# Per-head q and k transposes with per-head waits, in place of grouped loads with an early k, in a recurrent attention and FFN kernel

## The reference

```python
xn = layernorm(x)
q, k, v = heads(xn @ Wq), heads(xn @ Wk), heads(xn @ Wv)     # q, k rotated (rope)
beta = clip(sigmoid(xn @ Wg + bg), 0.8, 0.9995)
pq, pk = elu(q) + 1, elu(k) + 1
# for each token t and head:
S = S * b_t + pk_t (outer) v_t
z = z * b_t + pk_t
y_t = (pq_t @ S) / (sum(pq_t * z) + 1e-6)
s = y @ Wo + bo
# FFN with 8-bit weights, W = (wq - 128) * scale, hidden size 5632
g = silu( qlin( silu(qlin(xn, gate)) * qlin(xn, up), down ) )
out = x + s * g
```

## Time and profile before

| | us |
|---|---|
| two runs | 4832.46, 4834.73 |
| median of these | 4833.59 |
| the profiled execution | 4846.22 |
| its span, slowest core (2) | 4844.4 |
| its span, fastest core (5) | 4747.9 |

### The profile page before, as it was taken

The page is one execution under the profiler, slowest core; times in us unless marked ns, Lnnn a source line. Parts: engine busy times, 40 slices in busy tenths (PEclk is TensorE's granted clock), DMA queues, the critical chain, the costliest instruction groups (busy, mean ns, idle before and its releaser), DMA issues.

```text
span 4844.4 us, 44791 instructions; the slowest of 8 cores (4747.9 to 4844.4 us)
## 1 busy us (share of the span) xinstructions
PE 3282.6 (68%) x15312; PEld 1518.6 (31%) x15312; DVE 1009.8 (21%) x1735; ACT 528.2 (11%) x1021; POOL 632.2 (13%) x705
## 2 busy tenths in 40 slices
PE   0014777777761887877789888885525888638888
PEld 0012333323220433433334444443412333213333
DVE  1244435353521111111111111111400000000000
ACT  0110122222210111111111111111100000000000
POOL 0101243433320000000000000000010000100000
PEclk9997899999985988888899899897557899868899
DMA  7521132323229534355534453435394354764343
GB/s 147 140 87 23 38 75 47 79 46 78 45 67 208 114 93 114 88 116 114 105 85 106 91 118 92 91 83 122 100 161 112 105 131 125 136 129 120 104 130 96
DMA packets 661693, 491.81 MB, mean 102 GB/s; under 512 B 392928, under 2 KB 595680, under 8 KB 655328
## 3 DMA queue, kind: packets, MB, share of 16 engines
q0 software_dynamic: 67056, 173.10, 17.1%
q1 hardware_dynamic: 424944, 154.34, 14.6%
q10 hardware_dynamic: 169472, 161.52, 12.7%
HBM read 337.83 MB, written 167.77 MB: 104 GB/s over the span
## 4 chain that ended last, share of the span: by engine, by line
PE 48%; DMA 15%; DVE 11%; SPq 7%; POOL 7%; issue 7%; ACT 3%; ACTq 1%; DVEq 1%; POOLq 0%
PE pb L724 12%; PE pb L732 11%; PE pb L1060 10%; SPq L1006 6%; PE pb L985 5%; PE pb L581 4%; DMA raws<-wqu 4%; DMA raws<-wqg 4%; POOL swp L614 3%; DMA yTm<-yt_sp 2%; DMA raws<-wqd 2%; PE pb L856 2%; DVE tmp L628 2%; DVE tmp L620 2%; ACT mnb L626 2%
## 5 line engine op out<-in xcount | busy, mean ns | idle before, releaser
L724 PE MATMUL pb<-xnT,wgT 128*128 128x512 bf16 x2816 | 733.5, 420 | 104.0 <-DVE Am L805 70.9
L581 PE MATMUL pb<-ws,xnT 128*128 128x512 bf16 x2880 | 664.8, 392 | 115.0 <-DVE tmp L609 114.6
L732 PE MATMUL pb<-xnT,wuT 128*128 128x512 bf16 x2816 | 659.2, 389 | 103.9 <-DVE gub L745 87.0
L1060 PE MATMUL pb<-wdT,guTm 128*128 128x512 bf16 x2464 | 534.1, 379 | 0.0
L581 PEld LDWEIGHTS pb<-ws,xnT 128*128 128x128 bf16 x2880 | 284.4, 100 | 493.5 <-issue 188.3
L724 PEld LDWEIGHTS pb<-xnT,wgT 128*128 128x128 bf16 x2816 | 288.1, 106 | 479.5 <-issue 241.3
L732 PEld LDWEIGHTS pb<-xnT,wuT 128*128 128x128 bf16 x2816 | 280.3, 100 | 455.8 <-issue 139.2
L985 PE MATMUL pb<-wos,yTm 128*128 128x512 bf16 x960 | 272.5, 455 | 176.7 <-DMA yTm<-yt_sp 176.7
L1060 PEld LDWEIGHTS pb<-wdT,guTm 128*128 128x128 bf16 x2464 | 241.1, 98 | 290.7
L741 POOL TENSOR_TENSOR gub<-upsb,gsb 128x512 bf16<-128x512 bf16 x88 | 101.5, 1153 | 1235.0 <-ACT upsb L738 1234.8
L452 PE MATMUL pbt<-identb,xnb 128*128 128x128 bf16 x256 | 32.4, 306 | 337.2 <-DVE xnb L444 319.9
(11 more groups left out here) (110 smaller groups left out, 2200.3 us busy)
## 6 DMA issues: line engine op xcount, KB each, us to landing
guTm<-gu_sp ACTq DMA_DIRECT2D x64, 704.0 KB, 9.0
raws<-wqg POOLq DMA_DIRECT2D x11, 2048.0 KB, 19.0
wg_sp<-raws POOLq DMA_DIRECT2D x11, 2048.0 KB, 8.2
raws<-wqu POOLq DMA_DIRECT2D x11, 2048.0 KB, 15.5
wu_sp<-raws POOLq DMA_DIRECT2D x11, 2048.0 KB, 8.7
gu_sp<-gub ACTq DMA_DIRECT2D x176, 128.0 KB, 2.5
raws<-wqd POOLq DMA_DIRECT2D x16, 1408.0 KB, 13.3
wd_sp<-raws POOLq DMA_DIRECT2D x16, 1408.0 KB, 6.1
```

The costliest lines, as they stand in the source:

```text
L581: P.mm_group([(lambda e, k=k, m=m, sl=sl, pbank=pbank: e.matmul(pb[pbank][:, 0:512], xnT[:, k * L + m * 128:k * L + (m + 1) * 128], wslot[ ...
L724: P.mm_group([(lambda e, k=k, t=t, tb=tb, sl=sl: e.matmul(pb[6][:, 0:512], wgT[sl][:, k * FS + t * 128:k * FS + (t + 1) * 128], xnT[:, k * ...
L732: P.mm_group([(lambda e, k=k, t=t, tb=tb, sl=sl: e.matmul(pb[7][:, 0:512], wuT[sl][:, k * FS + t * 128:k * FS + (t + 1) * 128], xnT[:, k * ...
L1060: e.matmul(pb[pbank][:, 0:DDS], guTm[msl][:, kh * 256 + mi * 128:kh * 256 + (mi + 1) * 128], wdT[j][:, kh * DDS:(kh + 1) * DDS], start=(kh ...
```

## The change

The q and k loads of a group are written as eight single DMAs, q and k in turn for each head, at the start of the group. Each head's q and k has a buffer object and a semaphore of its own (`dqt0` to `dqt3`, `dkt0` to `dkt3`). The issue of the next group's k in chunk 15 is gone. `phase_A` consists of four matmul groups of one matmul, each waiting for its own head's q and k; numerator and denominator wait for all four heads. Tiles and arithmetic are the same.

```diff
-            qTgB, kTgB = P.buf("qTg"), P.buf("kTg")
+            qTgBh = [Buf(f"qTgh{hl}") for hl in range(HG)]
+            kTgBh = [Buf(f"kTgh{hl}") for hl in range(HG)]
...
-            def emit_q_loads(g):
-                P.dma_group("sp", [
-                    (lambda e, hl=hl, g=g: e.dma_start(
+            for g in range(NG):
+                for hl in range(HG):
+                    P.dma("sp", lambda e, hl=hl, g=g: e.dma_start(
                         qTg[:, hl * L:(hl + 1) * L],
-                        qt_sp[:, (g * HG + hl) * 128:(g * HG + hl + 1) * 128], transpose=True))
-                    for hl in range(HG)],
-                    reads=[qt_spB[m][g] for m in range(MT)], writes=[qTgB], sem="dqt")
-
-            def emit_k_loads(g):
-                P.dma_group("sp", [
-                    (lambda e, hl=hl, g=g: e.dma_start(
+                        qt_sp[:, (g * HG + hl) * 128:(g * HG + hl + 1) * 128], transpose=True),
+                        reads=[qt_spB[m][g] for m in range(MT)], writes=[qTgBh[hl]],
+                        sem=f"dqt{hl}")
+                    P.dma("sp", lambda e, hl=hl, g=g: e.dma_start(
                         kTg[:, hl * L:(hl + 1) * L],
-                        kt_sp[:, (g * HG + hl) * 128:(g * HG + hl + 1) * 128], transpose=True))
-                    for hl in range(HG)],
-                    reads=[kt_spB[m][g] for m in range(MT)], writes=[kTgB], sem="dkt")
-
-            for g in range(NG):
-                emit_q_loads(g)
-                if g == 0:
-                    emit_k_loads(0)
+                        kt_sp[:, (g * HG + hl) * 128:(g * HG + hl + 1) * 128], transpose=True),
+                        reads=[kt_spB[m][g] for m in range(MT)], writes=[kTgBh[hl]],
+                        sem=f"dkt{hl}")
...
-                    P.mm_group([(lambda e, hl=hl, c=c, bkA=bkA, kTg=kTg, qTg=qTg: e.matmul(
-                        pb[bkA][:, hl * 128:(hl + 1) * 128],
-                        kTg[:, hl * L + c * 128:hl * L + (c + 1) * 128],
-                        qTg[:, hl * L + c * 128:hl * L + (c + 1) * 128],
-                        start=True, stop=True)) for hl in range(HG)],
-                        reads=[qTgB, kTgB], writes=[pbB[bkA]])
+                    for hl in range(HG):
+                        P.mm_group([(lambda e, hl=hl, c=c, bkA=bkA: e.matmul(
+                            pb[bkA][:, hl * 128:(hl + 1) * 128],
+                            kTg[:, hl * L + c * 128:hl * L + (c + 1) * 128],
+                            qTg[:, hl * L + c * 128:hl * L + (c + 1) * 128],
+                            start=True, stop=True))],
+                            reads=[qTgBh[hl], kTgBh[hl]], writes=[pbB[bkA]])
...
-                    P.mm_group(numer_fns, reads=[stbB, qTgB, vchB[sl], AmB[cp]], writes=[pbB[bkN]])
+                    P.mm_group(numer_fns, reads=[stbB, vchB[sl], AmB[cp]] + qTgBh,
+                               writes=[pbB[bkN]])
...
-                    P.mm_group(den_fns, reads=[stbB, qTgB, AmB[cp], constsB], writes=[pbB[2]])
+                    P.mm_group(den_fns, reads=[stbB, AmB[cp], constsB] + qTgBh,
+                               writes=[pbB[2]])
...
-                    if c == NC - 1 and g + 1 < NG:
-                        emit_k_loads(g + 1)
```

More of the change, by code:

```diff
@@ L820, in phase_rest @@
                         h = g * HG + hl
-                        numer_fns.append(lambda e, hl=hl, h=h, c=c, bkN=bkN, qTg=qTg: e.matmul(
+                        numer_fns.append(lambda e, hl=hl, h=h, c=c, bkN=bkN: e.matmul(
                             pb[bkN][:, hl * 128:(hl + 1) * 128],
@@ L834, in phase_rest @@
                         h = g * HG + hl
-                        den_fns.append(lambda e, hl=hl, h=h, c=c, dco=dco, qTg=qTg: e.matmul(
+                        den_fns.append(lambda e, hl=hl, h=h, c=c, dco=dco: e.matmul(
                             pb[2][:, dco + hl:dco + hl + 1],
```

## The result

| | kernel before | changed kernel |
|---|---|---|
| median of the runs beside each other, us | 4838.7 | 4910.5 |
| ratio, with 95% interval | | 1.013 [1.0103, 1.0158] |
| profiled execution, us | 4846.2 | 4893.0 |
| its slowest core, span us | 2: 4844.4 | 7: 4891.4 |
| granted clock there | 0.859 | 0.858 |

Both medians include runs in which part of the chip ran at a lower clock; the ratio leaves such runs out, so it is the number to use. On the predicted base of 4833.6 it is +63 us, 50 to 76, or 4896 us; predicted were +53.6 and 4887. The change makes the kernel 1.3% slower, less than the 2% that the chances were put against.

What follows compares the result with a forecast made beforehand. TensorE's in-order stream in the recurrent stage was taken to bound the kernel. Late k 35.8, self-waits 14.8 and clock 3 summed to +53.6 us on 4833.6, giving 4887.2; own range 4875 to 4900, with rivals 4860 to 4924.

Steps and rivals of the forecast that it cites:

- part 1: At the three head-group changes, k leaves its early place, putting four transposes in the open each time: +35.8 us, bounds 28 to 59.
- Change 1: First head-group change: the raws load is over when the second four transposes start, so they go at the quiet rate, +11.4 us.
- Rival C: At the group changes, loads catch the added k transposes: +8 to +11 us at changes 1 and 3, 4905 to 4910; chance 0.15.
- Change 2: Second head-group change: the added four transposes fall into a raws load, FFN goes on 14 to 17 us later; taken as +13.
- The credit: At change 2: the 6.82 us stall for Am becomes short, and 2.7 us of lower clock behind it comes back.
- Change 3: Third head-group change, no FFN work left: k follows q at the quiet rate and everything after shifts, +11.4 us.
- The cover of the FFN weights: At change 2: wgT loads start up to 22 us later, yet end about 2853, before 2866.74, with 13 to spare.
- Part 2: phase_A in four groups, all 64 chunks: 192 self-waits of 0.32 us, partly covered by later waits, +14.8; bounds 8.6 to 61.
- Rival D: In phase_A, the self-wait is nearly free for 128-column matmuls: 36 to 38 us remain, 4871; chance 0.1.
- Part 3: FFN matmuls behind Am in 13 odd chunks: two fall to the lower clock, 2 x 1.7 = 3 us; bounds 0 and 35.
- Rival A: Self-waits drop the clock in most of 13 odd and six open even chunks: 32 to 51 us, about 4925; chance 0.1.
- Rival B: At the group changes, added transposes run beside the q ones for nothing, so not slower: 4835 or 4831; chance 0.04.

Runs made afterwards that it cites:

- e1: Changed kernel with phase_A as one matmul group again, so late k loads alone; ratio 1.0102 to the kernel before, stage +42 us.
- e8: Changed kernel with phase_A in one group and all four q transposes before the four k; ratio 1.0125 to the kernel before, stage +48 us.
- e5: Changed kernel with chunk 0's weight preparation put before chunk 1 instead, in groups 1 to 3; ratio 1.0138 to the kernel before.
- e11: Kernel before with preparation loads issued one job ahead, late k transposes and phase_A in one group; ratio 0.9856 to the kernel before.
- e2: Kernel before with phase_A in four groups, each waiting for TensorE's own count, loads unchanged; ratio 1.0022, stage +20 us.
- e3: Changed kernel without the waits for TensorE's own count in phase_A's matmuls 2 to 4; ratio 1.009 to the kernel before, stage +51 us.
- e12: Kernel before with preparation loads issued one job ahead and q transposed in two token halves, the first early; ratio 0.9631, median 4694 us.
- e7: Kernel before with each weight preparation's raws load issued one job ahead, into the other buffer; ratio 0.9813, stage -99 us.

## Why the prediction was right, and which step was mis-sized

**Direction and total: right.** Forecast +53.6, measured +63 [50, 76]. The mechanism was right too, with part 1 too small. The profiled execution was forecast at 4899.8 and took 4893.0.

**Part 1, the late k: right in kind, too small.** I had 35.8; e1 and e8, which have nothing else, give ratios of 1.0102 and 1.0125, 49 and 60 us, with a stage of +42 and +48. By changes:

- *Change 1, "+11.4": this is the step that failed.* The block grew by 21.9, and e1's stretch by 20.5. I had written that "the load is over by the time the second four start, so they go at the k rate", and against rival C that "DVE and POOL stand still in the stall, so no new load is issued". No new load is, but the store of the load before it is, and VectorE is free for the scaling that releases it. e5, which moves the store out, takes 5 to 8 of the extra 10 away, and in e11, where it falls on the load, the extra 10 doesn't appear. Rival C had the right mechanism at this one change (its +8 to +11), with the wrong transfer, and a smaller catch than its 13: 7.87 on core 1.
- *Change 2, "+13".* The added transposes came as worked out: predicted 19.4 to 22.4 more, measured 22.7. But FFN work went on 19.9 later by the median of eight cores, not 14 to 17, and the stretch in e1 grew by 22. The credit was too large: I took the stall for Am that goes away from the slowest core, 6.82, where the eight cores have 3.9 to 8.6, median 5.4. And the 2.7 of clock came back in part. Before, on core 2, the first gate group of the change took 5.30 and the second, behind the stall for Am, 6.32; in the changed kernel they took 5.48 and 3.61 on core 2, and 6.27 and 5.30 on core 7 (above). The second took 3.61 on six of the eight cores, and its median went from 5.30 to 3.61, so 1.7 came back. The rows of core 2, before and then changed:

```profile
2792.97 5.30 PE L724 MATMUL pb<-xnT,wgT 128*128 128x512 bf16 x16
```

```profile
2799.71 5.48 PE L724 MATMUL pb<-xnT,wgT 128*128 128x512 bf16 x16
...
2810.94 3.61 PE L724 MATMUL pb<-xnT,wgT 128*128 128x512 bf16 x16 [1.14 <-DVE Am L798]
```

- *Change 3, "+11.4".* Block +11.8, stretch +10.7 (+10.3 in e1). Right.
- The cover of the FFN weights held: on core 7 wgT was transposed from 2837.05 at 20.37, and the next span's came at 2911.77.

**Part 2, the self-waits: right.** 0.31 each instead of 0.32. Forecast 14.8, with 3 for the clock 17.8: by stage e2 costs 20, by its ratio 11 with an interval of -6 to 27, and taking the self-waits out of the change (e3) is worth 19 by the stage and 0.4% by the ratio, an amount that the two intervals don't tell from nothing. Rival D, a self-wait that is nearly free, fell with the 1.31 of every `phase_A`.

**Part 3, the clock: right, small.** The mean granted clock went from 0.859 to 0.858, the FFN gate matmuls' mean from 420 to 416 ns. By the medians of eight cores the mean stayed at 418 and 417. A few groups did fall, as core 1's at 2110.68, which took 5.30 after a wait of 1.08. Of the gate groups behind `phase_A` in the 13 odd chunks, 104 on eight cores, 15 took 5.30, 1.9 on a core where I had let two fall; 11 did in e2, and none before, in e1, in e3 and in e8. So it is the self-waits that do it. Rival A fell: nothing went down throughout. The Trainium skill (TensorE: Matmul & The Clock Gate, "A second HAM failure mode: psum-queue depth-cycling") has the clock swing in a kernel with frequent short idle times between groups of matmuls; here that is 15 groups of 104.

**Rival B** fell at once: the waits at changes grew by 51, not by nothing.

What stays open: one transpose now and then takes 20 to 40 us on one core, as the 30.02 of core 7 at change 1, which I can't tell ahead (the 66 in the expectation of e12 is a row of four, two of them long). In the profiled executions of the changed kernel, e1, e3, e5, e7 and e8 the slowest core has one. Whether the last 10 us between 53.6 and 63 are change 1 alone or in part such chances, the interval doesn't say.

## What to carry to other kernels

A load that is moved from an early place into a stall costs its full time there, and can collide with transfers that become free during the stall: list the loads and the stores of all queues, not just those issued at that moment. Price a small cost on the critical engine by whether a wait follows it in the same stretch; of the same 59 us of self-waits 22 were left with such waits behind them and 36 without. And before removing a wait, look for what it hides: here moving q gave 15 us of stage, loading ahead 99, and both together 153.

## What was unexpected of the hardware

- Waiting for TensorE's own count costs a matmul of 128 columns 0.31 us, as much as one of 512 columns (0.32): between these two the price doesn't depend on the columns. The Trainium skill (TensorE: Matmul & The Clock Gate, "The cost: per-tile semaphore tail") prices only the increments, about 26 ns each. By that figure three more of them would add an estimated 0.08; in e3, which keeps the increments and drops the waits, the four matmuls span 0.39 as before, so the row, in which matmul ends are modelled, shows none of it.
- A 2048 x 128 transpose takes about 2 to 6 us in a quiet queue (2.85 on average in the earlier trace rows), but the next one issued after GpSimd's 2 MB load is caught. At change 1 of the kernel before, the changed one, e1, e3, e5 and e8 the longest transpose took 11 to 16 in 37 of 48 cases, issued 0.4 to 2.7 after the load; in the other 11 it took 21 to 32. The load itself landed after 16 to 18 on seven of the eight cores before. It is one transpose that waits, not all that are slowed a little: its neighbours take 2 to 4. Beside the store one takes 6 to 13 (7.87 on core 1), and 20.56 where the store follows the load closely.
